# Linear attention written out by batch, with VectorE's work reordered and two out-projections joined

## The chip, the cores and the metric

The kernel runs on one core of a Trainium2 chip. The metric is the device time of one execution in microseconds. A core has five engines that work side by side and wait for each other through semaphores: TensorE (PE, matmuls), VectorE (DVE), ScalarE (ACT), GpSimd (POOL) and SyncE (SP, which issues the transfers). Each engine works through its own queue in program order.

## The reference

The input `x` has 8 batches of 1024 tokens with 256 features. Four layers follow each other, each on a layer-normalised input and added to `x`: softmax attention, a feed-forward layer (256 to 768, SiLU gate), gated linear attention with decay, and the same feed-forward layer again. The change is in the third, which computes with 8 heads of 64:

```python
q = _phi((x @ W_Q.T).reshape(b, t, H, DK))      # phi(u) = elu(u) + 1
k = _phi((x @ W_K.T).reshape(b, t, H, DK))
v = (x @ W_V.T).reshape(b, t, H, DK)
# for each token, in order:
S = g4 * S + jnp.einsum('bhi,bhj->bhij', kt, vt)
z = g3 * z + kt
num = jnp.einsum('bhij,bhi->bhj', S, qt)
den = jnp.sum(z * qt, axis=-1, keepdims=True) + EPS
# then
gate = jax.nn.sigmoid(x @ W_g_w.T + W_g_b).reshape(b, t, H, DK)
y = (outputs * gate).reshape(b, t, H * DK)      # outputs = num / den
return y @ W_O.T
```

## The kernel before

The stages run one after the other; linear attention is `linear_attention_phase`. It goes batch by batch, a batch in two halves of 512 tokens, a half in four chunks of 128 tokens.
**Projections.** Each half starts with 16 items on TensorE (`projection`, L1650): items 0 to 7 are query and key columns in turn, 8 to 11 the gate, 12 to 15 the values. Each item is six matmuls of 512 columns (L332, for the values L341), because weights and activations are kept as a high and a low part. The items go round four PSUM banks, `RING = (5, 2, 4, 3)`, and an item waits until the earlier contents of its bank have been read. ScalarE and VectorE turn items 0 to 7 into `phi` (L1481, L1483, then L1511), so item 11 needs the eighth `phi`. ScalarE takes the gate through tanh (L1487) and copies the values (L1491).

**VectorE in this part.** Between the `phi` operations stand: the decayed sums of the keys (`key_sums`, a scan, L1528), their product with the queries (`sums_by_query`, L1537), the statistics of the next half's layer norm (L132, L140), and two residual additions (L1580). After the eighth `phi` come the remaining two scans and products, the normalisation (L156) and a transpose of 32x32 blocks (L256). SyncE then moves the blocks to their places in 16 transfers (L271), ScalarE makes the high part (L276) and GpSimd the low part (L289, in two pieces) for the next half. TensorE's denominators (L1704) need all four products.

**GpSimd in this part** scales the queries (`qsT`, L1384, four times), and computes the layer norm's reciprocal root (L167, L170).

**Chunks.** For each chunk `c` TensorE's queue holds: the scores of the next chunk (L1693), the values under the decayed scores (`chunk_values`, L1734), the state's addition (`state`, L1757), the part of the earlier tokens (`earlier_values`, L1746), from `c = 2` on the out-projection of chunk `c - 2` (L1767, 12 matmuls), and the transposed keys of the next chunk (L1681). The out-projections of the last two chunks of a half stand behind items 2 and 5 of the next half. All of them go to bank 7.

VectorE gates a chunk's output (`gated`, L1574, into `yg`), ScalarE rounds it (`gated_high`, L1466), GpSimd subtracts (`gated_low`, L1448), and only then may the chunk's out-projection run. `yg`, `yg_hi` and `yg_lo` exist once each, so each step also waits for the step before of the next user. The state lives in `S`. GpSimd multiplies it by the decay (`decayed_state`, L1442) once the chunk's `earlier_values` have read it, and VectorE adds the new part (`update_state`, L1563, L1565). Chunks 0 and 7 of a batch need no decay, and chunk 7 no addition. On VectorE the order in chunk `c` is: decayed scores of the next chunk, `gated` of chunk `c - 1`, scaled keys (L1516), `update_state`, and from `c = 2` on `residual` of chunk `c - 2`, the addition to `x` that frees the out-projection's bank.

**The last half** also prepares the second feed-forward stage: layer norms of its next units, and `ff2_high` on GpSimd (L1436), which rounds its weights in pieces. The transfers of that half wait for all projections.

**Signals.** `signal.at(turn, k)` is the count at which `k` events of that turn have happened, so `x_done.at(b, 2)` means that the residuals of chunks 0 and 1 of batch `b` are done.

Of the kernel before, what the change touches and what calls it, by code (L numbers as in the profile page):

```python
# [1277 lines left out]
def linear_attention_phase(nc, block, env, io, front, following, signals, ff2_signals):  # L1278
# [6 lines left out]
    with ExitStack() as ctx:  # L1285
# [21 lines left out]
        yg_hi, yg_lo = sb("yg_hi", [P, NP, P], F32R), sb("yg_lo", [P, NP, P], F32R)  # L1307
# [6 lines left out]
        SPREAD_BANK = (6, 5, 7, 3)  # L1314
        NITEM = 3 * NP + UT
        NZERO = 4
# [34 lines left out]
        def run_batches(eng, turn):  # L1351
            turn(0, True, False)
            with eng.Fori(0, NB - 2) as p:
                turn(p + 1, False, False)
            turn(NB - 1, False, True)

        @block.sync
        def _(sp):
            sp.wait_ge(*env["ff1_down_end"])
            sp.dma_start(dist, io["dist"]).then_inc(const_loaded, 16)  # L1360
            sp.wait_ge(env["lin_lo"], LIN_PIECES)
            sp.wait_ge(prep_wo, 2)
# [9 lines left out]
            run_batches(sp, turn)  # L1372

        @block.gpsimd
        def _(pool):
            def turn(b, first, last):
                for half in range(NHALF):
                    if half > 0 or not first:
                        gated_low(b, UT * half - 1)
                    if first and half == 0:  # L1380
                        pool.wait_ge(decays, 1)
                    for j in range(NP):
# [5 lines left out]
                    nfront, n = next_of(b, half, last)  # L1388
                    nfront.ln.pool_rstd(pool, n)
                    for c in range(UT):  # L1390
# [3 lines left out]
                        if c == 2:  # L1394
                            nfront.pool_low_part(pool, n, 0, 0, landing_of(nfront))
                        if c > 0:
                            gated_low(b, UT * half + c - 1)
                        if c == 2:
                            nfront.pool_low_part(pool, n, 0, 1, landing_of(nfront))
# [45 lines left out]
            def gated_low(b, ch):  # L1445
                pool.wait_ge(yg_hi_done.sem, yg_hi_done.at(b, ch + 1))
                pool.wait_ge(out_ready.sem, out_ready.at(b, ch))
                nc.gpsimd.tensor_tensor(yg_lo[:], yg, yg_hi[:].bitcast(F32),  # L1448
                                        ALU.subtract).then_inc(yg_lo_done.sem, 1)
            run_batches(pool, turn)  # L1450

        @block.scalar
        def _(act):
# [9 lines left out]
            def gated_high(b, ch):  # L1463
                act.wait_ge(yg_done.sem, yg_done.at(b, ch + 1))
                act.wait_ge(out_ready.sem, out_ready.at(b, ch))
                nc.scalar.activation(yg_hi[:], yg, ACT.Copy).then_inc(yg_hi_done.sem, 1)  # L1466
# [34 lines left out]
            run_batches(act, turn)  # L1501

        @block.vector
        def _(dve):
# [72 lines left out]
            def residual(b, ch):  # L1577
                dve.wait_ge(out_ready.sem, out_ready.at(b, ch + 1))
                x = X[:, bass.ds(b * TB + ch, 1), :].rearrange("p a m -> p (a m)")
                nc.vector.tensor_tensor(x, PS[:, 7, 0:M], x, ALU.add).then_inc(x_done.sem, 1)  # L1580

            def turn(b, first, last):
                for half in range(NHALF):
# [5 lines left out]
                    for it in range(2 * NP):  # L1589
# [3 lines left out]
                        elif it in (4, 6):  # L1593
                            sums_by_query(b, half, it // 2 - 2)
                        elif it == 2 * NP - 1:
                            for j in range(NP // 2, NP):
                                key_sums(b, half, j)
                            for j in range(NP // 2, NP):
                                sums_by_query(b, half, j)
                        if it >= UT - 1 and it < 2 * UT - 1:  # L1600
                            nln.dve_tile_stats(dve, nturn, [it - (UT - 1)])
                        if it == 2 * UT - 2:
                            nln.dve_aggregate(dve, nturn)
                        if rest and it in (2, 5):
                            residual(b, c0 - 2 + it // 5)
                    nln.dve_normalise(dve, nturn)
                    nfront.dve_blocks(dve, nturn, (front, b * NHALF + half))
                    if first and half == 0:
# [8 lines left out]
                    inverse(b, half)  # L1617
                    for c in range(UT):
# [27 lines left out]
            run_batches(dve, turn)  # L1646

        def tensor(pe):
# [3 lines left out]
            def projection(b, half, it):  # L1652
# [108 lines left out]
            def out_projection(b, ch):  # L1761
                pe.wait_ge(yg_lo_done.sem, yg_lo_done.at(b, ch + 1))
                pe.wait_ge(x_done.sem, x_done.at(b, ch))
                parts = [(g[:, j, :], w[:, j, :]) for j in range(NP)
                         for g, w in ((yg_hi, w_o_hi), (yg_hi, w_o_lo), (yg_lo, w_o_hi))]
                for n, (g, w) in enumerate(parts):
                    last = nc.tensor.matmul(PS[:, 7, 0:M], g, w, start=n == 0, stop=n == len(parts) - 1)  # L1767
                last.then_inc(out_ready.sem, 1)

            def turn(b, first, last):  # L1770
                for half in range(NHALF):
# [21 lines left out]
                    for c in range(UT):  # L1793
# [18 lines left out]
            run_batches(pe, turn)  # L1812
# [98 lines left out]
```

## Time and profile before

| | us |
|---|---|
| median of 3 runs | 1885.44 (1884.46 to 1885.96) |
| the profiled execution | 1887.98 |
| its span, from the first to the last instruction | 1886.2 |

| engine | busy us | share of the span |
|---|---|---|
| TensorE, matmuls | 1829.4 | 97% |
| VectorE | 1355.4 | 72% |
| ScalarE | 881.6 | 47% |
| GpSimd | 605.5 | 32% |

The mean granted TensorE clock is 0.996 of full speed. The linear attention takes the stretch from about 820 to 1600 us. Busy shares are means over stages; what a change in one stage does is read from that stage's waits.

### The profile page before, as it was taken

To read this page: it belongs to the slowest core of one execution; us is meant where nothing else is said; L and a number is where in the kernel's file an instruction comes from. 1 tells how busy PE (TensorE), PEld (TensorE's weight loads), DVE (VectorE), ACT (ScalarE), POOL (GpSimd) and SP (SyncE) were. 2 spreads that over 40 slices of the span, in tenths; PEclk is the share of its full clock that TensorE was granted. 3 is DMA by queue.
4 is the path that set the end of the run, shared out by engine and by line. 5 is a ranking of instruction groups with operands and counts; after the bars stand their busy time and mean duration, and the time that the engine had idled before them with its cause. 6 is when DMAs were issued, how large, how long until landed. Compare 5 with 4: busy or idle time off the path is not lost.

```text
span 1886.2 us, 39692 instructions
## 1 busy us (share of the span) xinstructions
PE 1829.4 (97%) x14081; PEld 1548.4 (82%) x14081; DVE 1355.4 (72%) x2679; ACT 881.6 (47%) x1717; POOL 605.5 (32%) x541
## 2 busy tenths in 40 slices
PE   8999999999999999989999999999999998999998
PEld 7888888888888888878887878887878877888887
DVE  6566566556668888767776767676767777888885
ACT  6656656665554444453333333333333433444443
POOL 5313203311332222233434343334334435522211
PEclk9999999999999999999999999999999999999999
DMA  7100000000022122120000000000000001222322
GB/s 245 43 1 0 0 0 0 0 0 0 13 49 59 29 33 32 28 64 14 12 13 11 13 13 13 13 12 13 13 13 13 13 13 20 37 62 63 65 55 58
DMA packets 230679, 54.00 MB, mean 29 GB/s; under 512 B 209696, under 2 KB 228768, under 8 KB 230176
## 3 DMA queue, kind: packets, MB, share of 16 engines
q1 hardware_dynamic: 229296, 49.53, 13.0%
q10 hardware_dynamic: 1264, 2.76, 0.4%
q8 instruction: 90, 1.47, 0.3%
q14 instruction: 29, 0.24, 0.0%
HBM read 18.69 MB, written 8.39 MB: 14 GB/s over the span
## 4 chain that ended last, share of the span: by engine, by line
PE 80%; DVE 8%; issue 5%; POOL 3%; ACT 2%; SPq 1%; DMA 1%; DVEq 0%; ACTq 0%; POOLq 0%
PE PS L1213 17%; PE PS L332 10%; PE PS L1222 9%; PE PS L341 7%; PE PS L871 7%; PE PS L842 6%; PE PS L1693 4%; PE PS L860 3%; PE PS L1767 3%; PE PS L1746 3%; PE PS L1734 2%; PE PS L882 2%; DVE lin_zq L1528 2%; PE PS L1757 1%; SPq L271 1%
## 5 line engine op out<-in xcount | busy, mean ns | idle before, releaser
L332 PE MATMUL PS<-ln_xh,lin_w 128*128 128x512 f32 x768 | 254.2, 399 | 22.6 <-issue 11.8
L1145 ACT ACTIVATE ff_silu<-PS 128x512 f32<-128x512 f32 x192 | 114.4, 597 | 232.4 <-PE PS L1213 204.1
L1180 DVE SCALAR_TENSOR_TENSOR ff_h<-PS,ff_silu 128x512 f32<-128x512 f32 x192 | 131.2, 684 | 109.9 <-PE PS L1213 94.0
L332 PEld LDWEIGHTS PS<-ln_xh,lin_w 128*128 128x128 f32 x768 | 146.6, 191 | 62.2 <-DVE lin_kT L1511 16.8
L578 POOL TENSOR_TENSOR qk<-qk,swapped 64x128 f32<-64x128 f32 (+2 forms) x96 | 97.0, 1010 | 240.3 <-DVE swapped L722 234.4
L1164 DVE TENSOR_TENSOR ff_h_lo<-ff_h,ff_h_hi 128x512 fp32r<-128x512 f32 x192 | 165.3, 861 | 0.4
L1466 ACT ACTIVATE lin_yg_hi<-stage 128x512 fp32r<-128x512 f32 x64 | 40.4, 631 | 248.9 <-DVE stage L1574 133.8
L871 PE MATMUL PS<-probT,v_a 128*128 128x128 f32 x1152 | 153.3, 278 | 0.0
L332 PE MATMUL PS<-ln_xl,lin_w 128*128 128x512 f32 x384 | 152.1, 396 | 0.0
L871 PEld LDWEIGHTS PS<-probT,v_a 128*128 128x128 f32 x1152 | 139.5, 192 | 14.3 <-ACT probT L642 7.4
L842 PE MATMUL PS<-qk 128*128 128x512 f32 (+3 forms) x384 | 145.3, 489 | 1.0 <-POOL qk L578 0.9
L1442 POOL TENSOR_TENSOR lin_state<-lin_state,lin_decay_c 128x512 f32<-128x512 f32 x48 | 50.0, 1042 | 285.9 <-PE PS L1746 285.9
L732 DVE TENSOR_REDUCE neg_max<-PS 128x1 f32<-128x256 f32 (+7 forms) x128 | 95.7, 753 | 62.2 <-PE PS L845 61.0
L167 POOL TENSOR_SCALAR ln_var_eps<-ln_mean_var 128x4 f32<-128x4 f32 x64 | 15.1, 237 | 340.5 <-DVE ln_mean_var L140 340.5
L1131 ACT ACTIVATE ff_h_hi<-ff_h 128x512 fp32r<-128x512 f32 x192 | 119.5, 622 | 10.1 <-DVE ff_h L1180 10.1
L1384 POOL TENSOR_TENSOR lin_qsT<-lin_qT,lin_decay_q 128x512 f32<-128x512 f32 x64 | 98.8, 1560 | 66.1 <-DVE lin_qT L1511 56.1
L1448 POOL TENSOR_TENSOR lin_yg_lo<-stage,lin_yg_hi 128x512 fp32r<-128x512 f32 x64 | 81.8, 1279 | 98.1 <-ACT lin_yg_hi L1466 98.1
L1481 ACT ACTIVATE ln_xn<-PS 128x512 f32<-128x512 f32 x128 | 76.5, 598 | 77.1 <-PE PS L332 68.4
L1521 DVE TENSOR_TENSOR lin_AD<-PS,lin_decay 128x512 f32<-128x512 f32 x128 | 81.8, 680 | 30.5 <-PE PS L1693 29.5
L1222 PE MATMUL PS<-ff_w_hi,ff_h_hi 128*128 128x256 f32 x384 | 99.3, 291 | 3.8 <-issue 2.1
L632 ACT ACTIVATE prob<-PS,neg_max 128x256 f32<-128x256 f32 (+7 forms) x128 | 94.5, 738 | 14.1 <-DVE neg_max L732 10.5
L156 DVE TENSOR_SCALAR ln_xn<-X,ln_mean_var,ln_rstd 128x256 f32 (+1 forms) x256 | 98.8, 449 | 2.2 <-POOL ln_rstd L170 2.2
(194 smaller groups left out, 5279.7 us busy)
## 6 DMA issues: line engine op xcount, KB each, us to landing
ff_raw<-ln_xn SPq DMA_DIRECT2D x464, 32.0 KB, 2.0
lin_landing<-ln_xn SPq DMA_DIRECT2D x240, 32.0 KB, 2.0
out_x<-X SPq DMA_DIRECT2D x15, 512.0 KB, 2.9
X<-in_x SPq DMA_DIRECT2D x7, 1024.0 KB, 5.4
stage<-in_w_lin SPq DMA_DIRECT2D x1, 2048.0 KB, 8.2
stage<-in_w_gate SPq DMA_DIRECT2D x2, 768.0 KB, 7.2
stage<-in_w_up SPq DMA_DIRECT2D x2, 768.0 KB, 8.7
stage<-in_w_down SPq DMA_DIRECT2D x2, 768.0 KB, 10.1
```

Of the source, the lines that this page charges most:

```text
L156: last = nc.vector.tensor_scalar(out, x, self.mean_var[:, t, 0:1], self.rstd[:, t:t + 1], ALU.subtract, ALU.mult)
L332: last = nc.tensor.matmul(out, w, x, start=n == 0, stop=n == len(terms) - 1)
L341: last = nc.tensor.matmul(out, x[:, at], w, start=n == 0, stop=n == len(terms) - 1)
L842: last = nc.tensor.matmul(bank[:, 0:w], qk[:, 0, h, i * P:(i + 1) * P], qk[:, 1, h, c:c + w], start=True, stop=not diag)
L871: last = nc.tensor.matmul(O, V[:, j, h * DA:(h + 1) * DA], probT[:, n % 2, j, :], start=j == 0, stop=j == i)
L1131: nc.scalar.activation(h_hi[:, slot(par, f), :], h[:, f % 2, :], ACT.Copy).then_inc(hi_done.sem, 1)
L1145: nc.scalar.activation(silu[:, f % NB_GU, :], PS[:, f % NB_GU, :], ACT.Silu, scale=W_SCALE).then_inc(silu_done.sem, 1)
L1164: nc.vector.tensor_tensor(h_lo[:, slot(par, f), :], h[:, f % 2, :], h_hi[:, slot(par, f), :].bitcast(F32), ALU.subtract).then_inc(lo_done. ...
L1180: nc.vector.scalar_tensor_tensor(h[:, f % 2, :], PS[:, NB_GU + f % NB_GU, :], W_SCALE, silu[:, f % NB_GU, :], ALU.mult, ALU.mult).then_inc ...
L1213: ins = nc.tensor.matmul(PS[:, bank, :], w, x, start=n == 0, stop=n == len(parts) - 1)
L1222: ins = nc.tensor.matmul(Y[:, t // 2, (t % 2) * M:(t % 2 + 1) * M], a[:, slot(par, f), t * P:(t + 1) * P], w[:, f % NF, :], start=f == 0 a ...
L1384: nc.gpsimd.tensor_tensor(qsT[:, j, :].rearrange("p (c t) -> p c t", t=P), qT[:, j, :].rearrange("p (c t) -> p c t", t=P), Gq[:, j, :].uns ...
```

## The change

`run_batches` becomes a plain Python loop, so all eight batches are written out with constants. `yg_hi` and `yg_lo` are doubled, by the parity of the chunk. The out-projection of the second chunk of a half moves to the end of the third chunk, right behind that of the first, and goes to bank 5; item 0 of a half, the first to use bank 5, waits for its residual. On VectorE the statistics move into the first two `phi` items, the normalisation in front of the eighth `phi`, three of the four products behind the block transpose. On GpSimd the reciprocal root moves between the second and the third query scaling, and the low part of the next half's input, now one operation, from chunk 2 to chunk 1. In the last half the statistics of the following layer norm move ahead of the chunks, and its normalisation and transpose from chunk 1 to chunk 2.

```diff
-        yg_hi, yg_lo = sb("yg_hi", [P, NP, P], F32R), sb("yg_lo", [P, NP, P], F32R)
+        yg_hi, yg_lo = sb("yg_hi", [P, 2, NP, P], F32R), sb("yg_lo", [P, 2, NP, P], F32R)
...
-        SPREAD_BANK = (6, 5, 7, 3)
+        SPREAD_BANK, LOUT_BANK = (6, 5, 7, 3), (7, 5, 7, 7)
         NITEM = 3 * NP + UT
+        NORM_ITEM, LOW_CHUNK = 6, 1
...
-        def run_batches(eng, turn):
-            turn(0, True, False)
-            with eng.Fori(0, NB - 2) as p:
-                turn(p + 1, False, False)
-            turn(NB - 1, False, True)
+        def run_batches(turn):
+            for b in range(NB):
+                turn(b, b == 0, b == NB - 1)
...
# GpSimd
                     for j in range(NP):
                         pool.wait_ge(phi_done.sem, phi_done.at(b, 2 * NP * half + 2 * j + 1))
...
-                    nfront.ln.pool_rstd(pool, n)
+                        if j == 1:
+                            nfront.ln.pool_rstd(pool, n)
                     for c in range(UT):
                         decayed_state(b, UT * half + c)
...
-                        if c == 2:
-                            nfront.pool_low_part(pool, n, 0, 0, landing_of(nfront))
                         if c > 0:
                             gated_low(b, UT * half + c - 1)
-                        if c == 2:
-                            nfront.pool_low_part(pool, n, 0, 1, landing_of(nfront))
+                        if c == LOW_CHUNK:
+                            nfront.pool_low(pool, n, 0, landing_of(nfront))
...
             def gated_low(b, ch):
                 pool.wait_ge(yg_hi_done.sem, yg_hi_done.at(b, ch + 1))
-                pool.wait_ge(out_ready.sem, out_ready.at(b, ch))
-                nc.gpsimd.tensor_tensor(yg_lo[:], yg, yg_hi[:].bitcast(F32),
+                pool.wait_ge(out_ready.sem, out_ready.at(b, ch - 1))
+                nc.gpsimd.tensor_tensor(yg_lo[:, ch % 2], yg, yg_hi[:, ch % 2].bitcast(F32),
                                         ALU.subtract).then_inc(yg_lo_done.sem, 1)
...
# VectorE
-                        elif it in (4, 6):
-                            sums_by_query(b, half, it // 2 - 2)
-                        elif it == 2 * NP - 1:
-                            for j in range(NP // 2, NP):
-                                key_sums(b, half, j)
-                            for j in range(NP // 2, NP):
-                                sums_by_query(b, half, j)
-                        if it >= UT - 1 and it < 2 * UT - 1:
-                            nln.dve_tile_stats(dve, nturn, [it - (UT - 1)])
-                        if it == 2 * UT - 2:
+                        elif it == 4:
+                            sums_by_query(b, half, 0)
+                        if it < 2:
+                            nln.dve_tile_stats(dve, nturn, [2 * it, 2 * it + 1])
+                        if it == 2:
                             nln.dve_aggregate(dve, nturn)
                         if rest and it in (2, 5):
                             residual(b, c0 - 2 + it // 5)
-                    nln.dve_normalise(dve, nturn)
+                        if it == NORM_ITEM:
+                            nln.dve_normalise(dve, nturn)
+                    for j in range(NP // 2, NP):
+                        key_sums(b, half, j)
                     nfront.dve_blocks(dve, nturn, (front, b * NHALF + half))
+                    for j in range(1, NP):
+                        sums_by_query(b, half, j)
...
+                    if last and half == NHALF - 1:
+                        following.ln.dve_stats(dve, 1)
...
-                        if last and half == NHALF - 1:
-                            if c == 0:
-                                following.ln.dve_stats(dve, 1)
-                            if c == 1:
-                                following.ln.dve_normalise(dve, 1)
-                                following.dve_blocks(dve, 1, (following, 0))
+                        if last and half == NHALF - 1 and c == 2:
+                            following.ln.dve_normalise(dve, 1)
+                            following.dve_blocks(dve, 1, (following, 0))
...
# TensorE
                     pe.wait_ge(freed.sem, freed.at(b, k))
+                    if it == 0:
+                        pe.wait_ge(x_done.sem, x_done.at(b, c0 - 2))
...
             def out_projection(b, ch):
                 pe.wait_ge(yg_lo_done.sem, yg_lo_done.at(b, ch + 1))
-                pe.wait_ge(x_done.sem, x_done.at(b, ch))
+                pe.wait_ge(x_done.sem, x_done.at(b, ch if ch % UT == UT - 1 else ch - 1))
...
-                    last = nc.tensor.matmul(PS[:, 7, 0:M], g, w, start=n == 0, stop=n == len(parts) - 1)
+                    last = nc.tensor.matmul(PS[:, LOUT_BANK[ch % UT], 0:M], g, w, start=n == 0, stop=n == len(parts) - 1)
...
-                        if c >= 2:
+                        if c == 2:
                             out_projection(b, ch - 2)
+                            out_projection(b, ch - 1)
                         if c + 1 < UT and ch + 2 < NC:
                             keys(b, half, c + 1)
```

`gated_high` on ScalarE changes as `gated_low` does, and the residual on VectorE reads the bank that `LOUT_BANK` names.

## Rows read from the trace of the kernel before

**Rows 1.** Section 1 of the page: TensorE's busy time, share and instructions, with the others.

```profile
PE 1829.4 (97%) x14081; PEld 1548.4 (82%) x14081; DVE 1355.4 (72%) x2679; ACT 881.6 (47%) x1717; POOL 605.5 (32%) x541
```

**Rows 2.** TensorE's waits, 820 to 1600 us: total us, times, longest.

```profile
PE PS L332 <- issue: 11.8, 5, 2.6
PE PS L332 <- DVE lin_kT L1511: 9.7, 16, 1.7
PE PS L1757 <- DVE lin_state L1565: 7.1, 9, 2.2
...
PE PS L1718 <- issue: 0.8, 1, 0.8
```

**Rows 3.** The chain of waits at edges and the loop's end: start, us, what.

```profile
1106.49 2.06 issue
1108.55 5.99 PE PS L332 x18
...
1306.05 4.39 PE PS L332 x18
...
1499.58 4.11 PE PS L332 x18
```

**Rows 4.** Windows: stretch, length, busy of PE, PEld, DVE, ACT, POOL, clock, DMA.

```profile
1110.00:1112.00 2.00, 2.00 (x6) 1.52 (x6) 0.22 (x1) 1.23 (x2) 0.00 (x0) 0.50 0.00 0
...
1590.00:1593.00 3.00, 0.81 (x19) 0.70 (x18) 1.70 (x5) 1.06 (x1) 3.00 (x5) 1.00 0.07 11
```

**Rows 5.** The chain of waits, end of batch 6's first half.

```profile
1446.12 1.43 PE PS L1767 x12
...
1451.39 1.43 PE PS L1767 x12
1452.82 4.11 PE PS L332 x18
```

**Rows 6.** Timeline of GpSimd there: start, us, operation, count, idle before.

```profile
1446.20 1.04 POOL L1442 TENSOR_TENSOR lin_state<-lin_state,lin_decay_c 128x512 f32<-128x512 f32 x1 [1.83 <-PE PS L1746]
1447.20 1.27 POOL L289 TENSOR_TENSOR ln_xl<-lin_landing,ln_xh 128x512 fp32r<-128x512 f32 x1
1448.43 1.27 POOL L1448 TENSOR_TENSOR lin_yg_lo<-stage,lin_yg_hi 128x512 fp32r<-128x512 f32 x1
...
1451.47 1.04 POOL L1442 TENSOR_TENSOR lin_state<-lin_state,lin_decay_c 128x512 f32<-128x512 f32 x1 [0.54 <-PE PS L1746]
```

**Rows 7.** Timeline of VectorE at the boundary between the halves.

```profile
1452.55 0.86 DVE L1565 TENSOR_TENSOR lin_state<-PS,lin_state 64x256 f32<-64x256 f32 x2 [2.03 <-POOL lin_state L1442]
1453.44 0.42 DVE L1580 TENSOR_TENSOR X<-PS,X 128x256 f32 x1
```

**Rows 8.** Timeline of TensorE, second half of batch 6: item 11 and denominators.

```profile
1471.12 0.50 PE L332 MATMUL PS<-ln_xh,lin_w 128*128 128x512 f32 x1 [0.35 <-DVE lin_kT L1511]
...
1475.80 0.30 PE L1704 MATMUL PS<-lin_zq,lin_head_sum 128*32 128x128 f32 x2
```

**Rows 9.** Timeline of ScalarE: the eighth exponential of that half.

```profile
1467.32 0.63 ACT L1483 ACTIVATE ln_xn<-ln_xn 128x512 f32<-128x512 f32 x1
```

**Rows 10.** Groups by line, 915 to 1499 us: count, busy us, mean ns.

```profile
L156 DVE TENSOR_SCALAR ln_xn<-X,ln_mean_var,ln_rstd 128x256 f32 x48 | 16.5, 408 | 0.0
```

**Rows 11.** Timeline of VectorE: two scans and a product.

```profile
1315.20 1.22 DVE L1528 TENSOR_TENSOR_SCAN lin_zq<-lin_tmp_a,lin_kT 128x512 f32<-128x512 f32 x1
...
1461.69 2.35 DVE L1528 TENSOR_TENSOR_SCAN lin_zq<-lin_tmp_a,lin_z_last,lin_kT 128x512 f32<-128x512 f32 x1
...
1511.80 1.82 DVE L1537 TENSOR_TENSOR lin_zq<-lin_zq,lin_qT 128x512 f32<-128x512 f32 x1
```

**Rows 12.** Timeline of TensorE in batch 7's first half: items 10 and 11.

```profile
1516.98 0.50 PE L332 MATMUL PS<-ln_xh,lin_w 128*128 128x512 f32 x1 [0.71 <-DVE lin_qT L1511]
...
1520.34 0.50 PE L332 MATMUL PS<-ln_xh,lin_w 128*128 128x512 f32 x1 [1.71 <-DVE lin_kT L1511]
```

**Rows 13.** Timeline of ScalarE in the last half: the high part.

```profile
1590.90 1.06 ACT L276 ACTIVATE ln_xh<-ln_xl 128x1024 fp32r<-128x1024 f32 x1 [1.80 <-DMA ln_xl<-ln_xn]
```

More of the change, by code:

```diff
@@ L1370, in turn @@
                     nfront.sp_move(sp, n, 0, landing_of(nfront))
-            run_batches(sp, turn)
+            run_batches(turn)
         @block.gpsimd
@@ L1381, in turn @@
                         pool.wait_ge(decays, 1)
+                    nfront, n = next_of(b, half, last)
                     for j in range(NP):
@@ L1387, in turn @@
                                                 ALU.mult).then_inc(qs_done.sem, 1)
-                    nfront, n = next_of(b, half, last)
-                    nfront.ln.pool_rstd(pool, n)
+                        if j == 1:
+                            nfront.ln.pool_rstd(pool, n)
                     for c in range(UT):
@@ L1446, in gated_low @@
                 pool.wait_ge(yg_hi_done.sem, yg_hi_done.at(b, ch + 1))
-                pool.wait_ge(out_ready.sem, out_ready.at(b, ch))
-                nc.gpsimd.tensor_tensor(yg_lo[:], yg, yg_hi[:].bitcast(F32),
+                pool.wait_ge(out_ready.sem, out_ready.at(b, ch - 1))
+                nc.gpsimd.tensor_tensor(yg_lo[:, ch % 2], yg, yg_hi[:, ch % 2].bitcast(F32),
                                         ALU.subtract).then_inc(yg_lo_done.sem, 1)
-            run_batches(pool, turn)
+            run_batches(turn)
         @block.scalar
@@ L1464, in gated_high @@
                 act.wait_ge(yg_done.sem, yg_done.at(b, ch + 1))
-                act.wait_ge(out_ready.sem, out_ready.at(b, ch))
-                nc.scalar.activation(yg_hi[:], yg, ACT.Copy).then_inc(yg_hi_done.sem, 1)
+                act.wait_ge(out_ready.sem, out_ready.at(b, ch - 1))
+                nc.scalar.activation(yg_hi[:, ch % 2], yg, ACT.Copy).then_inc(yg_hi_done.sem, 1)
             def turn(b, first, last):
@@ L1499, in turn @@
                     gated_high(b, TB - 1)
-            run_batches(act, turn)
+            run_batches(turn)
         @block.vector
@@ L1579, in residual @@
                 x = X[:, bass.ds(b * TB + ch, 1), :].rearrange("p a m -> p (a m)")
-                nc.vector.tensor_tensor(x, PS[:, 7, 0:M], x, ALU.add).then_inc(x_done.sem, 1)
+                nc.vector.tensor_tensor(x, PS[:, LOUT_BANK[ch % UT], 0:M], x, ALU.add).then_inc(x_done.sem, 1)
             def turn(b, first, last):
@@ L1644, in turn @@
                     residual(b, TB - 1)
-            run_batches(dve, turn)
+            run_batches(turn)
         def tensor(pe):
@@ L1762, in out_projection @@
                 pe.wait_ge(yg_lo_done.sem, yg_lo_done.at(b, ch + 1))
-                pe.wait_ge(x_done.sem, x_done.at(b, ch))
-                parts = [(g[:, j, :], w[:, j, :]) for j in range(NP)
+                pe.wait_ge(x_done.sem, x_done.at(b, ch if ch % UT == UT - 1 else ch - 1))
+                parts = [(g[:, ch % 2, j, :], w[:, j, :]) for j in range(NP)
                          for g, w in ((yg_hi, w_o_hi), (yg_hi, w_o_lo), (yg_lo, w_o_hi))]
                 for n, (g, w) in enumerate(parts):
-                    last = nc.tensor.matmul(PS[:, 7, 0:M], g, w, start=n == 0, stop=n == len(parts) - 1)
+                    last = nc.tensor.matmul(PS[:, LOUT_BANK[ch % UT], 0:M], g, w, start=n == 0, stop=n == len(parts) - 1)
                 last.then_inc(out_ready.sem, 1)
@@ L1810, in turn @@
                     rest_of_last.update({0: lambda: out_projection(b, TB - 2), 2: lambda: out_projection(b, TB - 1)})
-            run_batches(pe, turn)
+            run_batches(turn)
             return rest_of_last
```

## The prediction

> **What bounds the kernel now.** The page's first section says it: TensorE is busy 97% of the span [rows 1]. So I looked for what makes TensorE wait, in the stage that the diff touches, linear attention, from about 820 to 1600 us. The list of waits there [rows 2] is short: 11.8 us in five waits put down to "issue", 9.7 us in 16 waits for `kT`, 7.1 us in 9 waits for the state's update. The chain of waits places the five: each stands at the back-edge of the loop over batches 1 to 6 [rows 3]. The edge has an after-effect. The 18 matmuls of the three items behind it take 4.11 us where no edge stands before them, 5.96 to 5.99 us behind three of the edges and 4.37 to 4.39 us behind the other two [rows 3]; behind such an edge the granted clock is 0.50, the lower level, 1.2 GHz [rows 4].
>
> Because TensorE has little idle time, every new wait in its queue lengthens the run unless it replaces an old one. The rest of the work is therefore to follow its queue through one half of a batch. T is the start of a half's first projection item.
>
> **The loop written out.** All five back-edges go: 11.8 us of waiting, and 3 x 1.87 + 2 x 0.27 = 6.1 us of slow matmuls, together 17.9. With them goes the pipelining that a stop breaks, about 0.15 us each (an estimate: 12 matmuls of 0.28 us take 1.43 us together in [rows 5], so one starts 0.16 before the end of the one ahead, and the waits are counted from that end), so -18.6. The straight-line end of the loop shows no wait at all before its items, which is what an unrolled boundary looks like [rows 3], its line at 1499.58. Bounds: -18.6 as the whole of it; where the next wait takes part of it over, that stands with that wait below.
>
> **The join of out-projections 0 and 1 of a half.** Before, chunk 2 ends with out-projection 0 and chunk 3 with number 1; now both stand at the end of chunk 2. What TensorE does there is in [rows 5]: out-projection 0 starts at 1446.12 and takes 1.43 us. Number 1 needs `yg_lo` of chunk 1. GpSimd decays the state first, which may start only when the earlier-values matmuls of chunk 2 end, at the same moment: L1442 at 1446.20, 1.04 us, then L1448, 1.27 us [rows 6]. Even with nothing between, `yg_lo` is there at 1446.20 + 1.00 + 1.27 = 1448.5 and TensorE is free at 1447.5: a wait of 1.0 us. Now GpSimd's whole `pool_low` (two L289 of 1.25 us, 2.5 together) has been moved ahead of that decay, to chunk 1. There GpSimd is done with `yg_lo` of chunk 0 at about 1444.35 (L1448 runs one decay after chunk 1's earlier values), so `pool_low` ends at 1446.85 and the decay starts 0.65 late: 1.65 us. Its input is not late, because the block transposes start earlier in the half than before. I take 1.6 us for a first half and 1.4 for a second, which has a short wait of 0.1 us at that spot already: 8 x 1.6 + 7 x 1.4 = +22.6; ends +14 (1.0 in all 15, less the old 0.1 in seven) and +26. The old waits for the state's update (7.1 us, [rows 2]) stay outside the last half: keys 3 move behind both projections, and the same chain of key scaling and update follows them.
>
> **Bank 5 for out-projection 1.** It makes a new wait: item 0 of the next half writes bank 5, so it waits for `x_done` of chunk 1. On VectorE that residual stands behind `update_state` of chunk 3, and this behind GpSimd's decay, which waits for chunk 3's earlier values. Before, 1.43 us of out-projection and then the items covered this chain; now the earlier values are the last thing TensorE does in the half. The chain is in the rows: earlier values end at 1451.39 [rows 5], decay from 1451.47 [rows 6], update from 1452.55, residual at 1453.44 for 0.42 us [rows 7], done at 1453.86. That is 2.5 us of empty TensorE, 2.7 with the lost overlap. Queued behind it are all 16 items, and ScalarE's and VectorE's chains start from them, so nothing takes it back later. In a second half chunk 7 has no state update, and the residual is ready in time; so eight boundaries: 8 x 2.7 = +21.6, ends +19 and +23. No row gives it below zero, since the order on the three queues is fixed.
>
> **VectorE's new order in the projections.** TensorE's last gate item needs the eighth `phi`. Item by item for a second half (T = 1452.82): it is free for that item at 1471.12 - 0.35 = T + 17.95 [rows 8], ScalarE delivers the last exponential at 1467.95 = T + 15.1 [rows 9]. Before, four statistics, an aggregate, two sums and two products stood ahead of the eighth `phi`. Now one product less and the four normalisations more (4 x 0.35, [rows 10] gives 0.41 for one alone), with statistics and aggregate in the gaps before the fourth `phi`. From the fourth `phi` at T + 8.85: first scan to 11.1 (2.35 with GpSimd in its way) or 10.0 (1.22) [rows 11]; fifth `phi` 0.6; product 0.6, or 1.8 when it meets GpSimd [rows 11]; sixth 0.6; scan 1.2 to 2.3; residual 0.35; seventh 0.6; normalise 1.4; eighth 0.6. That is T + 16.4 to 19.2, against 17.95: a wait of 0 to 1.3. Then two scans 2.3, the transpose 1.2, three products 1.8 (2.3 in a first half, with their copies): 22.3 to 25.0. The denominators, which need them, come at 1475.80 - 0.35 = T + 22.7 [rows 8] plus the first wait: 0 to 1.0 more. I take 1.2 us for a first half and 0.5 for a second, 13.6 in all, against 9.7 of [rows 2] less what batch 0 has extra: +5. Ends: -9.7 (all of these waits gone) and +27 (2.3 us in all 16). A row in between: the batch behind the loop, whose start is not delayed, waits 0.71 + 1.71 us in a first half in the old order [rows 12], where the 16 waits of [rows 2] are 0.6 on average, so part of the edge's gain is taken over there; the new order would turn that 2.4 into about 1.2 to 1.9.
>
> The Trainium skill's "SBUF — State Buffer", section "Who interferes with whom", says that VectorE with two SBUF inputs and GpSimd lock each other out for a whole instruction, in order of issue. The two scans of [rows 11] agree (1.22 and 2.35 us). If every scan and product ahead of the eighth `phi` lost that race, this term would be at its +27; with all races won it would be negative.
>
> **The last half.** The transpose's input there comes late whatever the order (the moves wait for all projections): L276 runs at 1590.90 to 1591.96 [rows 13]. GpSimd's `pool_low` now stands ahead of `ff2_high` and the decay of chunk 6: 1591.96 + 2.5 + 2.4 + 1.0 + 1.3 = 1599.2 for `yg_lo` of chunk 5. Out-projection 5 and then chunk 7's values, 1.4 + 2.1, end at 1602.8, against about 1600.7 before; the earlier statistics save only waits ahead of that. +3 with what the feed-forward start adds, ends 0 and +8.
>
> **Double `yg_hi` and `yg_lo`.** They take away waits of ScalarE and GpSimd for the previous out-projection. `yg` itself stays single, so VectorE still waits for `yg_lo`. Off the path: 0. Without the doubling the join would wait longer still.
>
> **Clock.** Stops of 2.06, 2.54 and 2.55 us were followed by the lower level, 2.26 and 2.41 us were not, and each fall cost 1.87 [rows 3, 4]. Eight new stops of 2.5 us, each with shorter ones before it: I take three or four falls, +6, ends 0 and 8 x 1.87 = +15.
>
> **Sum.** -18.6 + 22.6 + 21.6 + 5 + 3 + 6 = +39.6 us. On the profiled execution's 1887.98 that is 1927.6. The median of the runs is 2.5 below that execution, so I forecast 1925 for a median (+2.1%). The ends of the unknown terms with the firm ones: -18.6 + 14 + 19 - 9.7 + 0 + 0 = +5, so 1890; all upper ends together +82, which I don't think can coincide; terms one by one put the upper end near +58, 1944.
>
> **The rivals.** *A, faster: the edge's gain outweighs the waits.* Its place is the joined projections and bank 5. If `yg_lo` of chunk 1 and the residual of chunk 1 are there when TensorE comes, only edges and `phi` waits are left: -18.6 - 9.7 = -28, 1857; half of the new waits paid gives about 1879. It decides for faster once join and bank together cost under 18 us, 1.1 us per half. For it: TensorE's stops at the edges are plain in [rows 3]. Against it: the chains of [rows 5 to 7] have fixed order and durations. 17%.
> *B, about even (within 0.2%).* Phi waits vanish, clock never falls, join costs its lower end: +5 and less, 1886 to 1890. 6%.
> *C, slower by much more.* After each stop the clock falls, twice per half: the Trainium skill's "TensorE: Matmul & The Clock Gate", section "HAM oscillation — how this bites in real kernels", says that repeated idling keeps the clock low. Priced by rows: 8 x 1.87 = 15 for the boundaries and perhaps as much for the joins, so 1885.4 + 33.6 + 30 = 1949. For it: three of five edges fell. Against it: in the last half TensorE was busy for 0.81 us of three and the granted clock stayed 1.00 [rows 4]. 12%.
> *D, the written-out code pays for its own fetching.* Then "issue" waits appear inside batches. The list has 0.8 us of it once outside the edges, and batches 0 and 7 are straight [rows 2]. 3%, about +10 more.
> My forecast with its own terms: 62%.
>
> From these: faster by over 0.2% 0.17, within 0.2% 0.05, slower 0.78; 0.2% is about what a measurement of this kernel can tell from no change. Range 1884 to 1944.
>
> **What would show it.** In the changed profile: no "issue" wait before L332 (edges right); in each first half a wait of about 2.5 us at item 0, released by VectorE's residual L1580-equivalent (bank 5 right); about 1.5 us before the second out-projection, released by GpSimd's `yg_lo` (join right); waits of 0 to 1.3 us for `kT` and up to 1 us before the denominators (VectorE's order right). A median under 1885 would mean that one of the two chains is shorter than the old rows say, or is not met.

## The result: 1946.1 us, slower by 3.2%

| | us |
|---|---|
| median after (4 runs) | 1946.14 (1941.96 to 1947.31) |
| median before (4 runs) | 1885.7 |
| ratio | 1.0316, 95% interval 1.0298 to 1.0333 |
| profiled execution after, before | 1945.9, 1887.98 |

The forecast was 1925 with a range to 1944: the direction was right, the size too small by a third, and the time lies just outside the range. Section 1 of the page after, against [rows 1]:

```profile
PE 1844.4 (95%) x14081; PEld 1558.9 (80%) x14081; DVE 1360.3 (70%) x2679; ACT 878.0 (45%) x1717; POOL 583.7 (30%) x525
```

The instruction count on TensorE is the same. Its busy time grew by 15 us, mostly slow matmuls, and the rest of the 58 us between the two profiled executions is standing still. All waits of TensorE from 820 to 1660 us (total us, times, longest), against [rows 2]:

```profile
PE PS L1766 <- POOL lin_yg_lo L1446: 27.9, 16, 6.3
PE PS L332 <- DVE X L1578: 21.5, 8, 2.7
PE PS L332 <- DVE lin_kT L1509: 12.0, 16, 6.6
PE PS L1703 <- DVE lin_AD L1535: 11.4, 15, 1.0
PE PS L1756 <- DVE lin_state L1563: 4.9, 8, 0.6
```

Lines have moved: L1766 is the out-projection, L1578 the residual, L1703 the denominators, L1446 `gated_low`, L1440 the state's decay; they move again in each experiment. The waits called issue are gone. In their place stand the join's (27.9) and bank 5's (21.5). GpSimd's timeline in the first half of batch 1 (start, us) answers to [rows 6]:

```profile
963.22 1.28 POOL L1446 TENSOR_TENSOR lin_yg_lo<-stage,lin_yg_hi 128x512 fp32r<-128x512 f32 x1
964.46 2.38 POOL L281 TENSOR_TENSOR ln_xl<-lin_landing,ln_xh 128x1024 fp32r<-128x1024 f32 x1
966.80 1.04 POOL L1440 TENSOR_TENSOR lin_state<-lin_state,lin_decay_c 128x512 f32<-128x512 f32 x1
967.80 1.26 POOL L1446 TENSOR_TENSOR lin_yg_lo<-stage,lin_yg_hi 128x512 fp32r<-128x512 f32 x1
```

Low part, decay and `yg_lo` follow each other without a gap, and the second out-projection starts at 969.11, after 1.43 us of waiting. The chain of waits over the boundary that follows, against [rows 5, 7]:

```profile
974.73 1.05 POOL lin_state L1440
...
975.88 0.42 DVE lin_state L1563
...
976.30 0.43 DVE lin_state L1563
976.73 0.03 issue
976.76 0.44 DVE X L1578
977.20 0.14 issue
977.33 5.89 PE PS L332 x18
```

Decay, update, residual, and then TensorE's first items, which take 5.89 us instead of 4.11. The windows show why (columns as in [rows 4]):

```profile
975.00:977.00 2.00, 0.00 (x0) 0.00 (x0) 1.08 (x3) 0.00 (x0) 1.99 (x2) 1.00 0.00 0
977.00:979.00 2.00, 1.67 (x4) 1.41 (x5) 0.82 (x2) 0.00 (x0) 0.00 (x0) 0.56 0.00 0
979.00:981.00 2.00, 2.00 (x6) 1.55 (x6) 0.00 (x0) 0.70 (x2) 0.00 (x0) 0.58 0.00 0
981.00:983.00 2.00, 2.00 (x10) 1.67 (x9) 1.35 (x3) 1.60 (x3) 0.00 (x0) 1.00 0.00 0
```

TensorE is empty for two microseconds, and then the granted clock is at its lower level, 1.2 GHz, for most of the next four. This happened at all eight boundaries: 5.88 to 5.96 us six times and 7.17 to 7.18 twice, 17.0 us above 8 x 4.11.

### The profile page after: what moved, and what is told of

Its sections match the earlier page's. It is cut to its first block, busy times and chain, and to the rows that moved or that the text cites. A ratio compares the mean times of both kernels' runs of the same rounds, so it can differ in the third digit from the quotient of the medians.

```text
span 1944.1 us, 38598 instructions
## 1 busy us (share of the span) xinstructions
PE 1844.4 (95%) x14081; PEld 1558.9 (80%) x14081; DVE 1360.3 (70%) x2679; ACT 878.0 (45%) x1717; POOL 583.7 (30%) x525
## 4 chain that ended last, share of the span: by engine, by line
PE 60%; issue 16%; DVE 10%; POOL 9%; SPq 2%; ACT 2%; DMA 1%; ACTq 0%; DVEq 0%; POOLq 0%
PE PS L1213 16%; PE PS L1222 9%; PE PS L332 9%; PE PS L871 7%; PE PS L842 6%; PE PS L341 4%; PE PS L860 3%; DVE lin_zq L1526 3%; POOL lin_state L1440 3%; PE PS L882 2%; POOL lin_yg_lo L1446 2%; SPq L271 2%; PE PS L1766 2%; POOL ln_xl L281 1%; DVE lin_kT L1509 1%
## 5 line engine op out<-in xcount | busy, mean ns | idle before, releaser
L332 PE MATMUL PS<-ln_xh,lin_w 128*128 128x512 f32 x768 | 262.9, 412 | 33.4 <-DVE X L1578 21.5
L332 PEld LDWEIGHTS PS<-ln_xh,lin_w 128*128 128x128 f32 x768 | 152.0, 198 | 73.2 <-issue 22.8
L1440 POOL TENSOR_TENSOR lin_state<-lin_state,lin_decay_c 128x512 f32<-128x512 f32 x48 | 49.9, 1041 | 370.6 <-PE PS L1745 370.6
L332 PE MATMUL PS<-ln_xl,lin_w 128*128 128x512 f32 x384 | 156.1, 406 | 0.0
L167 POOL TENSOR_SCALAR ln_var_eps<-ln_mean_var 128x4 f32<-128x4 f32 x64 | 28.3, 442 | 325.6 <-DVE ln_mean_var L140 325.6
L1446 POOL TENSOR_TENSOR lin_yg_lo<-stage,lin_yg_hi 128x512 fp32r<-128x512 f32 x64 | 81.6, 1275 | 128.1 <-ACT lin_yg_hi L1464 128.1
L156 DVE TENSOR_SCALAR ln_xn<-X,ln_mean_var,ln_rstd 128x256 f32 (+1 forms) x256 | 111.9, 500 | 6.0 <-POOL ln_rstd L170 6.0
L1766 PE MATMUL PS<-lin_w_o_hi,lin_yg_hi 128*128 128x256 f32 x256 | 75.9, 296 | 29.4 <-POOL lin_yg_lo L1446 29.4
L1222 PE MATMUL PS<-lin_w,ff_h_hi 128*128 128x256 f32 x384 | 98.4, 289 | 2.5 <-issue 2.5
```

The source lines that it names most:

```text
L156: last = nc.vector.tensor_scalar(out, x, self.mean_var[:, t, 0:1], self.rstd[:, t:t + 1], ALU.subtract, ALU.mult)
L332: last = nc.tensor.matmul(out, w, x, start=n == 0, stop=n == len(terms) - 1)
L1222: ins = nc.tensor.matmul(Y[:, t // 2, (t % 2) * M:(t % 2 + 1) * M], a[:, slot(par, f), t * P:(t + 1) * P], w[:, f % NF, :], start=f == 0 a ...
L1446: nc.gpsimd.tensor_tensor(yg_lo[:, ch % 2], yg, yg_hi[:, ch % 2].bitcast(F32), ALU.subtract).then_inc(yg_lo_done.sem, 1)
L1766: last = nc.tensor.matmul(PS[:, LOUT_BANK[ch % UT], 0:M], g, w, start=n == 0, stop=n == len(parts) - 1)
```

## The experiments

Each kernel ran beside the kernel before on the same chip. Ratios are against that, with their 95% intervals.

**1. Writing out alone** (`unroll_only`): the kernel before, with

```diff
-            turn(0, True, False)
-            with eng.Fori(0, NB - 2) as p:
-                turn(p + 1, False, False)
-            turn(NB - 1, False, True)
+            for b in range(NB):
+                turn(b, b == 0, b == NB - 1)
```

> The kernel before with its eight linear-attention batches written out and nothing else. Theory (the extra time of the change comes from waits in TensorE's queue and the clock behind them, none of it from writing the batches out): the five edges go (-18.6 us), and part comes back as waits for the eighth phi in the five first halves that started late until now, which then look like batch 7's (2.4 us instead of 0.76, +1.66 each, +8): about 1876 us, no wait called issue before an item. Rival (straight code costs instruction fetching): issue waits inside the batches, 1886 us or more.

Measured: 1882.64 us, ratio 0.9986 (0.9977 to 0.9996). TensorE's first three waits:

```profile
PE PS L332 <- DVE lin_kT L1509: 15.8, 16, 2.0
PE PS L1755 <- DVE lin_state L1563: 7.1, 9, 2.2
PE PS L332 <- DVE lin_qT L1509: 5.3, 8, 0.7
```

No issue wait, so the rival falls. But the gain is 3 us, not 10. The edges' 18.6 us went, and 10.3 came back as waits for `phi` (15.8 + 5.3, before 9.7 + 1.1), as expected. In one batch (1123 to 1129 us) the clock also fell behind the two waits of 0.70 and 1.99 us, and once more at the start of the feed-forward stage, where the kernel before has no fall:

```profile
1129.00:1131.00 2.00, 2.00 (x17) 1.79 (x16) 1.93 (x6) 0.69 (x1) 0.13 (x1) 0.50 0.00 0
1603.00:1605.00 2.00, 2.00 (x12) 2.00 (x11) 2.00 (x1) 1.97 (x3) 2.00 (x1) 0.50 0.00 0
```

Two falls are some 3.6 us, an estimate from the 1.8 us of a fall. That is one execution: the ten runs of this kernel have mean granted clocks of 0.997 (this one) to 1.0, so the number of falls differs between executions of the same program. What is left of the difference stays open.

**2. The join undone** (`join_undone`): the changed kernel with out-projection 1 back in chunk 3, in bank 7, and without the wait of item 0.

```diff
-        SPREAD_BANK, LOUT_BANK = (6, 5, 7, 3), (7, 5, 7, 7)
+        SPREAD_BANK, LOUT_BANK = (6, 5, 7, 3), (7, 7, 7, 7)
...
-                    if it == 0:
-                        pe.wait_ge(x_done.sem, x_done.at(b, c0 - 2))
...
-                        if c == 2:
+                        if c >= 2:
                             out_projection(b, ch - 2)
-                            out_projection(b, ch - 1)
```

> The changed kernel with the out-projections back at their old places and all in bank 7, without the new wait of item 0; VectorE's and GpSimd's new orders, the doubled gated parts and the written-out batches stay. Theory: the 16 waits for yg_lo (27.9 us), the 8 for the residual (21.5) and the slow clock behind them (17) go: 1946 - 66 = 1880 us. Rival (the clock is low for another reason, such as the phi and denominator waits): the waits go and the slow matmuls stay, about 1897 us.

Measured: 1884.12 us, 0.9994 (0.9984 to 1.0003): 62.0 us under the changed kernel, all that the change had lost. All 15 later groups of three items take 4.11 us. So the join with its bank carries the whole loss, and the other parts of the change cancel each other. The waits of 0.3 to 1.0 us for `phi` and the denominators, which stay, don't bring the clock down. The two long ones do: it is low behind the wait of 6.7 us in batch 0 and that of 5.1 us in the last half.

**3. The join alone** (`join_alone`): `unroll_only` with the join, its bank, its wait and the doubled parts, in GpSimd's old order.

```diff
...
+                    if it == 0:
+                        pe.wait_ge(x_done.sem, x_done.at(b, c0 - 2))
...
-                        if c >= 2:
+                        if c == 2:
                             out_projection(b, ch - 2)
+                            out_projection(b, ch - 1)
```

> The written-out kernel before (unroll_only, 1882.6 us) with the join alone: doubled gated parts, out-projection 1 behind number 0 into bank 5, item 0 waiting for its residual. GpSimd's order is the old one, in which the decay and the first piece of the low part stand ahead of yg_lo. Theory (order in the queues sets the waits): 15 waits of 2.2 us for yg_lo (33), 8 of 2.7 for the residual (21.5), 17 of slow clock: about 1954 us. Rival (the join is harmless, and VectorE's new order made the loss): 1883 to 1890 us.

Measured: 1954.84 us, 1.0358 (1.0340 to 1.0376). Its first two waits:

```profile
PE PS L1767 <- POOL lin_yg_lo L1446: 32.9, 15, 2.2
PE PS L332 <- DVE X L1578: 21.5, 8, 2.7
```

15 x 2.2 = 33, as read from the old GpSimd order. The change's own order of GpSimd made the join cheaper, not dearer. The forecast of 1954 came out partly by luck. The waits for `phi` are 4.3 us shorter than in experiment 1, and the clock fell more often than the eight times behind the 17 us. Here it also fell behind the join's stop of 2.2 us, in six of the eight first halves and one of the seven second ones (out-projection 1 of batch 0 starts at 862.26):

```profile
862.00:864.00 2.00, 1.74 (x10) 1.75 (x11) 0.00 (x0) 0.00 (x0) 1.44 (x2) 0.71 0.00 0
864.00:866.00 2.00, 2.00 (x12) 1.67 (x13) 0.36 (x1) 0.00 (x0) 0.00 (x0) 0.50 0.00 0
```

Behind the boundaries it fell seven times of eight, in six of these for the second time within some 10 us.

**4. The residual ahead of the update** (`residual_early`), on VectorE in chunk 3:

```diff
+                        if c == 3:
+                            residual(b, ch - 2)
                         if ch + 1 < NC:
                             update_state(b, ch)
-                        if c >= 2:
+                        if c == 2:
                             residual(b, ch - 2)
```

> The changed kernel with one move on VectorE: in chunk 3 the residual of chunk 1 stands ahead of the state's update, so item 0 of the next half no longer waits for GpSimd's decay. Theory (the wait of item 0 makes the clock fall): -21.5 for the wait and -17 for the clock, 1908 us, and the three first items of every second half take 4.1 us. Rival (the clock falls from the sum of all waits of a half): -21.5 alone, 1925 us, with 5.9 us for these items.

Measured: 1907.48 us, 1.0120 (1.0103 to 1.0137), 38.7 us under the changed kernel. The wait of 21.5 us is gone, and each second half begins with items of 4.12 or 4.13 us. The 15 waits of 1.44 us and eight of 0.6 that are left do not lower the clock by themselves.

**5. The wait filled** (`wait_filled`):

```diff
                     if it == 0:
+                        if half == 1:
+                            for _ in range(11):
+                                nc.tensor.matmul(PS[:, KEY_BANK, :], w_hi[:, 0, 0:P], sx.hi[:, 0, :], start=True, stop=True)
                         pe.wait_ge(x_done.sem, x_done.at(b, c0 - 2))
```

> The changed kernel with 11 matmuls of 512 columns, whose result nobody reads, ahead of item 0's wait in every second half. They fill the 2.7 us in which TensorE stood empty. Theory (idleness at this place lets the clock fall): the wait itself is not shortened, only the 17 us of slow matmuls go, 1929 us. Rival (the clock falls for another reason): 1946 us, unchanged, or slower by what the extra matmuls overrun.

Measured: 1934.05 us, 1.0262 (1.0244 to 1.0279), 12.1 us less with more work. The boundary in its timeline (TensorE, start and us):

```profile
972.52 1.16 PE L1748 MATMUL PS<-lin_qsT,lin_state 128*128 128x128 f32 x8
973.44 2.77 PE L1660 MATMUL PS<-ln_xh,lin_w 128*128 128x512 f32 x11
976.28 0.50 PE L332 MATMUL PS<-ln_xh,lin_w 128*128 128x512 f32 x1
```

Item 0 still starts after the residual, now with TensorE busy until then, and the three items take 4.37 to 4.42 us. Of the 17.0 us, 8 x 0.28 = 2.3 is left; the other 14.7 us were the clock. The clock falls because TensorE stands still here. The run is 5 us above the forecast of 1929; 2.3 of these are that rest, and in the last half the wait for `yg_lo` was 7.2 us instead of 6.3.

**6. `yg_lo` ahead of the decay** (`low_before_decay` on top of 4, `low_alone` on the changed kernel), on GpSimd in chunk 2:

```diff
+                        if c == 2:
+                            gated_low(b, UT * half + c - 1)
                         decayed_state(b, UT * half + c)
...
-                        if c > 0:
+                        if c in (1, 3):
                             gated_low(b, UT * half + c - 1)
```

> residual_early, with GpSimd's gated_low of chunk 1 ahead of the state's decay in chunk 2. Theory (out-projection 1 waits for 1.44 us because yg_lo stands behind that decay and pool_low): yg_lo is ready about 0.85 us earlier, 15 waits of 0.6 us instead of 1.44, 1907.5 - 12.5 = 1895 us. Rival (the decay that is now late makes the state's update late, and the wait moves there): the waits for the state grow by as much, 1907 us or more.

Measured: 1894.99 us, 1.0046 (1.0030 to 1.0061), 12.5 under experiment 4. The waits for `yg_lo` fall from 29.4 to 16.9 us, and those for the state's update stay at 4.9.

> The changed kernel with gated_low of chunk 1 ahead of the decay, and the residual left behind the state's update: TensorE stops for 0.6, 0.6 and 2.7 us around the middle of a batch instead of 1.44, 0.6 and 2.7. Theory A (the stop of 2.7 us at the boundary alone decides on the clock): all eight falls stay, 5.9 to 7.2 us for the three items behind it, 1946 - 12.5 = 1933.5 us. Theory B (the shorter stops a few us before count as well): fewer falls, as behind the loop's edges (three of five), some 6 to 8 us less, 1926 us.

Measured: 1925.58 us, 1.0211 (1.0194 to 1.0228): theory B, whose number was 1926. The 8 waits for the residual are the same, 21.5 us, but their effect alternates. The chain, at four boundaries in a row:

```profile
974.80 4.36 PE PS L332 x18
...
1074.62 5.97 PE PS L332 x18
...
1176.06 4.35 PE PS L332 x18
...
1275.86 5.96 PE PS L332 x18
```

Four falls instead of eight, and 8.4 us instead of 17.0. So a stop of 2.7 us was followed by the lower clock nearly always where one of 1.44 us or more stands some 6 us ahead of it (8 of 8 in the changed kernel, 7 of 8 in `join_alone` and in `root_first` below), and every other time where that one is 0.6 us. By itself (experiment 4) the stop of 1.44 us has no such effect. That the shorter stop is the cause is not shown. Within this one trace the same stops went both ways, so something else decides as well. The move also shortened the time from one such boundary to the next, from 103.5 to 100.7 us on average, and no run changed the stop and kept the time.

**7. The root ahead of the tables** (`root_first`), in batch 0 on GpSimd:

```diff
+                    nfront, n = next_of(b, half, last)
                     if first and half == 0:
+                        nfront.ln.pool_rstd(pool, n)
                         pool.wait_ge(decays, 1)
-                    nfront, n = next_of(b, half, last)
...
-                        if j == 1:
+                        if j == 1 and not (first and half == 0):
                             nfront.ln.pool_rstd(pool, n)
```

> The changed kernel, where in the first half of batch 0 alone GpSimd computes the reciprocal root ahead of its wait for the decay tables. Theory (the 6.6 us for kT in batch 0 come from the normalisation, which now stands ahead of the eighth phi and so behind GpSimd's wait for tables that ScalarE makes after its last exponential): -6.6 and some 2 us of slow clock behind it, 1937 us. Rival (this wait is VectorE's own load, as in the other halves): unchanged, 1946 us.

Measured: 1940.89 us, 1.0294 (1.0278 to 1.0310), 5.2 us less. The wait of 6.6 us is gone; one of 2.5 before that half's denominators took part of its place. Between the two traces that half is 4.2 us shorter. From there on the queues are those of the changed kernel, with the same stops of 1.44, 0.6 and 2.7 us, and still the clock did not fall at one of the eight boundaries:

```profile
1179.52 4.36 PE PS L332 x18
```

In the changed kernel VectorE's normalisation shows what it stood behind:

```profile
828.83 0.67 DVE L1509 SCALAR_TENSOR_TENSOR lin_qT<-PS,ln_xn 128x512 f32<-128x512 f32 x1
834.24 3.26 DVE L156 TENSOR_SCALAR ln_xn<-X,ln_mean_var,ln_rstd 128x256 f32<-128x256 f32 x4 [4.75 <-POOL ln_rstd L170]
837.42 0.68 DVE L1509 SCALAR_TENSOR_TENSOR lin_kT<-PS,ln_xn 128x512 f32<-128x512 f32 x1
```

GpSimd waited for the tables until 830.38, then scaled two queries and computed the root. The eighth `phi` (837.42) came behind all of it.

**8. A version that beats both** (`sums_first`): experiment 2, with the normalisation and the transpose behind all products again, and in the last half the low part in chunk 2.

```diff
...
-                        if it == NORM_ITEM:
-                            nln.dve_normalise(dve, nturn)
                     for j in range(NP // 2, NP):
                         key_sums(b, half, j)
-                    nfront.dve_blocks(dve, nturn, (front, b * NHALF + half))
                     for j in range(1, NP):
                         sums_by_query(b, half, j)
+                    nln.dve_normalise(dve, nturn)
+                    nfront.dve_blocks(dve, nturn, (front, b * NHALF + half))
```

> join_undone (1884.1 us), with VectorE's normalisation and transpose behind all products again (the statistics stay in the gaps of the first two phi), and in the last half GpSimd's low part in chunk 2 again. Theory (the four normalisations and the transpose ahead of the eighth phi and of the products are what TensorE waits for): the 15 waits for the denominators (11.1), those for kT (5.6 outside batch 0) and the 6.7 us of batch 0 go, and about 5 us of the last half: 1884 - 26 = 1858 us, faster than both kernels. Rival (VectorE and GpSimd lock each other out on the scans, whatever the order): the eighth phi still comes late, 1870 us or more.

Measured: 1853.92 us, 0.9823 (0.9809 to 0.9836), 1.8% faster than before. No wait for `phi` is left, and 0.7 us before a denominator once:

```profile
PE PS L1753 <- DVE lin_state L1563: 6.0, 8, 1.7
PE PS L1763 <- POOL lin_yg_lo L1446: 4.2, 2, 3.8
...
PE PS L1700 <- DVE lin_AD L1535: 0.7, 1, 0.7
```

The normalisation ahead of the eighth `phi` and the transpose ahead of the products, moved back together, were what cost: 30.2 us against experiment 2, with the low part of the last half. What pays against experiment 1, 28.7 us, was not taken apart. The statistics in the gaps of the first items, three products instead of two behind the eighth `phi`, GpSimd's root between the query scalings, its low part in chunk 1 and the doubled parts all differ.

**9. The same with the loop** (`sums_first_looped`), `run_batches` as before:

```diff
-            for b in range(NB):
-                turn(b, b == 0, b == NB - 1)
+            turn(0, True, False)
+            with eng.Fori(0, NB - 2) as p:
+                turn(p + 1, False, False)
+            turn(NB - 1, False, True)
```

> sums_first (1853.9 us) with the hardware loop over batches 1 to 6 again. Theory (writing the batches out saves the five edges, and their gain was only hidden in unroll_only by waits for the eighth phi, which this VectorE order doesn't have): +18 us, about 1872 us. Rival (the edges cost little by themselves, as unroll_only's 3 us say): 1857 us.

Measured: 1868.10 us, 0.9903 (0.9885 to 0.9921), 14.2 us above experiment 8. TensorE's first wait is that of the edges:

```profile
PE PS L332 <- DVE stage L1574: 10.2, 5, 2.2
```

The profile puts these stops down to VectorE and not to issue. The clock fell behind those of 2.02, 2.12 and 2.15 us and not behind those of 1.70 and 2.21. From the second half of batch 0 to that of batch 7 the two traces differ by 17.2 us (664.6 against 647.4); the runs of each kernel spread over about 7 us. By the medians, written-out batches are worth nearly five times as much here as in experiment 1. That nothing else is late at the boundary fits this, and was not tested apart.

## Why the prediction was wrong in size and right in mechanism

| term | forecast us | measured us | from |
|---|---|---|---|
| edges | -18.6 | -14.2 | experiments 8, 9, medians |
| join, 15 halves | +22.6 | +20.9 | 27.9 - 6.3 - 0.7 |
| bank 5 | +21.6 | +21.5 | waits after |
| `phi` and denominators | +5 | +4.1 | 5.4 + 11.4 - 9.7 - 1.1 - 1.9, without batch 0's 6.6 |
| batch 0's tables | 0 | +5.2 | experiment 7 |
| last half, feed-forward start | +3 | +6.6 | 8.4 from its start to the end in both traces, less 1.8 of clock in the next row |
| clock at the boundaries | +6 | +17.0 | chain after |

The measured column adds up to 61.1, the medians differ by 60.4 and the profiled executions by 57.9. So close a sum is partly luck, since the edges come from two other kernels and the rest from single traces. In the traces the stage also begins 3.3 us earlier after. Its start lies between 816.4 and 819.7 us in all twelve traces, with nothing changed ahead of it, so this is the scatter of single executions.

- **Edges.** They went, and no fetching took their place (rival D falls). Of the 18.6 us, 17.2 show between the traces of experiments 8 and 9 and 14.2 between their medians; with the old VectorE order it was 3. The part of the text that the next wait takes a share over was right, and too small for `unroll_only`.
- **Join and bank 5.** Both chains came as read, to 0.2 us: 1.44 us where 1.4 to 1.6 was forecast, 2.68 where 2.7 was. Experiments 2, 4 and 6 show them by taking them away, and experiment 3 by adding them. Rivals A and B fall.
- **Clock: the step that failed most.** "I take three or four falls, +6" took about half of the new stops to be followed by a fall, after the edges' three of five. All eight were, and two falls were longer than any before (3.1 us instead of 1.8): 17.0 us, more than even the upper end of +15. Experiments 4 and 5 show that TensorE's standing still for 2.7 us is what these falls need. Why they came eight times of eight and not half of the time stays open. Ahead of each stood stops of 1.44 and 0.6 us, ahead of the edges only one of 0.1, and with 0.6 us in place of 1.44 (experiment 6) it was four of eight. But the same stops went both ways in experiments 6 and 7, so their lengths do not decide alone. Rival C was right that the clock falls at every boundary. It was wrong for the changed kernel's joins of 1.44 us and mostly right for the first halves' joins of 2.2 us in experiment 3.
- **VectorE's order.** The waits of 0.30 and 0.41 for the eighth `phi` and of 0.56 and 1.00 for the denominators lie inside the ends of 0 to 1.3 and 0 to 1.0. The normalisation took 2.35 us in every half behind the first, where the working had 1.4. But the working was for a half in the middle. It missed that in batch 0 the root had been moved behind GpSimd's wait for the tables, and the normalisation ahead of a `phi`: 6.6 us of waiting, 5.2 of time by the medians of experiment 7. This term stood at nothing in the sum.
- **Last half.** The wait before out-projection 5 is 6.3 us, at 1650.23, from the chain that the text names (moves, low part, weight rounding, decay). Up to the first matmul of the feed-forward stage the half is 4.9 us longer (56.3 against 51.4), of which 1.8 is the clock at its boundary and 3.1 the forecast's +3. From there to the end it is 3.6 us more, and that the working had left nearly out: 3.2 us of waiting for the first `ff_h` (0.7 before), and slow matmuls behind it. The 3.2 us stand in experiments 2 and 8 as well, and experiment 3 has 0.7, so they come from the new orders of the other engines and not from the join. Which of them was not tested.

The clock missed by 11.0 us, batch 0 by 5.2, the edges by 4.4 and the last half by 3.6; the join came 1.7 lower and the `phi` row 0.9. With 0.1 less for bank 5 that makes 21.5. The medians differ by 20.8 more than the forecast's +39.6. Two small slips in the working change nothing: all its upper ends add up to +80, not +82, and the lower end of the eighth `phi` to T + 16.0, not T + 16.4.

## What to carry to other kernels

When TensorE is busy 97% of the time, a matmul group moved earlier must be checked against the chain that makes its input, and a PSUM bank newly shared against everything that stands ahead of its reader on the reader's engine: both could be read to 0.2 us from the trace of before. Price the clock as well. A stop of 2.0 to 2.7 us cost another 1.8 us, sometimes 3.1, where the clock fell behind it, and its length did not tell whether it would. So take a fall at every such stop as the upper end. Taking the stop away is better: moving one residual ahead of one update returned 39 us. Follow a reordered queue through the first and the last iteration too, and test a loop written out also in an order in which little else is late.

## What the runs showed of the hardware that was not expected

- The length of a stop of TensorE did not tell whether the granted clock would fall behind it. At the loop's edges it fell behind stops of 2.06, 2.54 and 2.55 us and not behind 2.26 and 2.41 (before), behind 2.02, 2.12 and 2.15 and not behind 1.70 and 2.21 (experiment 9). A stop of 2.7 us behind 1.44 or 2.2 and 0.6 us was followed by a fall 22 of 24 times (three kernels), behind 0.6 and 0.6 us 4 of 8 times. The stops of 1.44 and 0.6 us without the long one were not, in any of the boundaries of experiment 4. A fall cost 1.8 us, or 3.1 in three cases. Filling the stop with unread matmuls took all eight falls away.
- VectorE's normalisation, with one tensor input in SBUF, is also held up by GpSimd. The four together took 1.38 us before with GpSimd idle, and 2.35 us beside a query scaling, in every half but the first:

```profile
1474.54 1.38 DVE L156 TENSOR_SCALAR ln_xn<-X,ln_mean_var,ln_rstd 128x256 f32 x4
...
1512.56 2.35 DVE L156 TENSOR_SCALAR ln_xn<-X,ln_mean_var,ln_rstd 128x256 f32<-128x256 f32 x4
...
1512.72 1.39 POOL L1384 TENSOR_TENSOR lin_qsT<-lin_qT,lin_decay_q 128x512 f32<-128x512 f32 x1 [2.07 <-DVE lin_qT L1509]
```

The Trainium skill's "SBUF — State Buffer", section "Who interferes with whom", lists this operation, `tensor_scalar`, among those that can take the shared pair. The forecast's 1.4 us had not used this.
